# The index add moved to the head of GpSimd's chunk, and the first chunk's field loads split and reordered

## The reference

```python
e = jnp.stack([tbl_0[ids[:, 0]], ..., tbl_38[ids[:, 38]]], axis=1)      # (2048, 39, 16)
x0 = xk = e
for idx, (W, b) in enumerate(params):                                   # three layers, 128 outputs each
    z = jax.nn.relu(jnp.einsum('bhd,bkd,hks->bsd', x0, xk, W) + b[None, :, None])
    if idx != n_layers - 1:
        half = z.shape[1] // 2
        xk = z[:, :half, :]
        direct.append(z[:, half:, :])
    else:
        direct.append(z)
z = jnp.sum(jnp.concatenate(direct, axis=1), axis=-1)
h = jnp.concatenate([z, dense_ctx], axis=1)
h = jnp.maximum(h @ W_top1 + b_top1, 0.0)
h = jnp.maximum(h @ W_top2 + b_top2, 0.0)
y = h @ W_top3
```

## Time and profile before

| | |
|---|---|
| Time, median of 3 runs | 2474.45 us (2474.23 to 2475.2) |
| The profiled execution | 2474.38 us, of it the span 2472.6 us |
| TensorE (PE) busy | 2373.9 us, 96% |
| TensorE weight loads (PEld) | 1539.6 us, 62% |
| VectorE (DVE) busy | 2212.4 us, 89% |
| ScalarE (ACT) busy | 1364.1 us, 55% |
| GpSimd (POOL) busy | 2155.9 us, 87% |
| DMA, mean over the span | 189 GB/s |
| Granted TensorE clock, mean | 0.995 |

### The profile page before, as it was taken

How to read it: one execution, slowest core, us unless ns; L and a number is a source line. 1 busy time by engine, 2 the same in 40 slices (tenths; PEclk the granted TensorE clock), 3 DMA queues, 4 the chain that set the end, 5 groups by cost and what they waited for, 6 DMA issues and landing times. The chain is left out here.

```text
span 2472.6 us, 32417 instructions
## 1 busy us (share of the span) xinstructions
PE 2373.9 (96%) x8192; PEld 1539.6 (62%) x8192; DVE 2212.4 (89%) x2047; ACT 1364.1 (55%) x1532; POOL 2155.9 (87%) x1350
## 2 busy tenths in 40 slices
PE   1799999999999999999999999999999999999999
PEld 1466666666666666666666666666666666666665
DVE  2689999999999999999999999999999999999983
ACT  2355555555555555555555555555555555555552
POOL 4799999999999999999999999999999999999640
PEclk9899999999999999999999999999999999999999
DMA  7888888888878888888888788888888878888710
GB/s 179 187 187 207 196 185 211 212 173 209 207 186 194 210 209 176 204 211 181 203 204 209 177 204 212 181 206 205 201 180 208 214 177 208 208 188 191 199 55 1
DMA packets 398547, 467.04 MB, mean 189 GB/s; under 512 B 170337, under 2 KB 179553, under 8 KB 398257
## 3 DMA queue, kind: packets, MB, share of 16 engines
q1 hardware_dynamic: 299202, 302.30, 54.3%
q10 hardware_dynamic: 78848, 159.39, 24.7%
q0 software_dynamic: 20480, 5.15, 1.8%
HBM read 457.03 MB, written 9.71 MB: 189 GB/s over the span
## 5 line engine op out<-in xcount | busy, mean ns | idle before, releaser
L458 POOL TENSOR_TENSOR low<-prod_pool,high 128x1024 fp32r<-128x1024 f32 (+1 forms) x640 | 1532.5, 2395 | 88.8 <-ACT high L775 73.2
L775 ACT ACTIVATE high<-prod_pool 128x1024 fp32r<-128x1024 f32 (+1 forms) x640 | 677.3, 1058 | 733.5 <-DVE prod_pool L516 695.9
L627 PE MATMUL z<-prod_whole,w_whole 128*128 128x512 f32 (+1 forms) x2176 | 1011.5, 594 | 5.6 <-DVE prod_whole L516 5.6
L627 PE MATMUL z<-high,w_high 128*128 128x512 f32 (+1 forms) x1920 | 939.5, 489 | 55.9 <-ACT high L775 55.9
L627 PE MATMUL z<-high,w_low 128*128 128x512 f32 (+1 forms) x1920 | 758.6, 395 | 0.0
L429 POOL DMA_INDIRECT rows<-table,index x640 | 611.5, 955 | 147.8 <-issue 99.0
L516 DVE TENSOR_TENSOR prod_whole<-xh,x 128x1024 f32<-128x1024 f32 x512 | 620.5, 1212 | 110.1 <-PE z L627 90.8
L627 PE MATMUL z<-low,w_high 128*128 128x512 f32 (+1 forms) x1920 | 614.0, 401 | 33.5 <-POOL low L458 33.3
L627 PEld LDWEIGHTS z<-prod_whole,w_whole 128*128 128x128 f32 (+1 forms) x2176 | 412.7, 190 | 355.7 <-issue 296.8
L516 DVE TENSOR_TENSOR prod_pool<-xh,x 128x1024 f32<-128x1024 f32 x512 | 621.3, 1213 | 10.0 <-POOL low L458 10.0
L627 PEld LDWEIGHTS z<-high,w_high 128*128 128x128 f32 (+1 forms) x1920 | 363.6, 189 | 229.2 <-issue 141.1
(11 more groups left out here) (45 smaller groups left out, 365.5 us busy)
## 6 DMA issues: line engine op xcount, KB each, us to landing
xh<-x_rows SPq DMA_DIRECT2D x64, 2560.0 KB, 16.5
xh<-x_rows ACTq DMA_DIRECT2D x64, 2432.0 KB, 20.6
xb<-x_rows SPq DMA_DIRECT2D x128, 546.0 KB
xb<-x_rows SPq DMA_DIRECT2D x64, 468.0 KB
xa<-x_rows SPq DMA_DIRECT2D x192, 78.0 KB
rows<-table,index POOLq DMA_INDIRECT x640
x_rows<-rows SPq DMA_DIRECT2D x256, 20.0 KB
xh<-staged SPq DMA_DIRECT2D x2, 1280.0 KB, 6.9
```

Source lines behind the costliest of these rows:

```text
L458: pool.tensor_tensor(low[0:g.rows, g.split_slot, 0:n, :], prod_pool[0:g.rows, g.slot, 0:n, :], high[0:g.rows, g.split_slot, 0:n, :].bitcas ...
L627: return pe.matmul(z[stage][:, :], weights[0:g.rows, table[stage, t], :], src[0:g.rows, i, :], start=t == 0 and weights is not w_low and s ...
L775: act.activation(high[0:g.rows, g.split_slot, 0:n, :], src[0:g.rows, 0:n, :], ACT.Copy).then_inc(high_ready, 1)
```

## The change

Two things, both in the order of work and in what is waited for; no computation is added or dropped.

First, `begin_gather` is cut in two. `make_index` holds the waits for the ids and for the stored rows and the add; it runs at the head of GpSimd's chunk, before the first low part. `begin_gather` keeps the wait for the add's semaphore and runs where it ran. Chunk 0 makes two indices; only the first one moves.

Second, in chunk 0 alone: ScalarE copies xa before it asks for the odd fields, no longer after; odd and even fields are each asked for in two parts, tiles 0 to 9 and the rest, with a semaphore of its own for the first parts (`first_fields_loaded`); VectorE starts stage 1 when the first parts are in, and waits for the rest at the group that begins with tile 10.

```diff
+        first_fields_loaded = sem("first_fields_loaded")
...
-        def load_fields(engine, c, p, hh):
+        def load_fields(engine, c, p, hh, loaded, first=0, end=TK):
...
-            n = (F + 1 - hh) // 2
-            spread = bass.AP(tensor=col.tensor, offset=col.offset + hh * step,
-                             ap=[[0, H], [2 * step, n], [1, CN]])
-            engine.dma_start(xh[p][hh * H:(hh + 1) * H, 0:n, :], spread).then_inc(xh_loaded[p], 16)
+            end = min(end, (F + 1 - hh) // 2)
+            spread = bass.AP(tensor=col.tensor, offset=col.offset + (2 * first + hh) * step,
+                             ap=[[0, H], [2 * step, end - first], [1, CN]])
+            engine.dma_start(xh[p][hh * H:(hh + 1) * H, first:end, :], spread).then_inc(loaded, 16)
+
+        def load_first_fields(engine, hh):
+
+            load_fields(engine, 0, 0, hh, first_fields_loaded, end=TK // 2)
+            load_fields(engine, 0, 0, hh, xh_loaded[0], first=TK // 2)
...
-                load_fields(sp, c, p, 0)
+                if known and c == 0:
+                    load_first_fields(sp, 0)
+                else:
+                    load_fields(sp, c, p, 0, xh_loaded[p])
...
-            def begin_gather(c, p):
-
-
+            def make_index(c, p):
                 pool.wait_ge(ids_loaded[p], 8 * (c - p) + 16)
+                if not isinstance(c, int) or c >= 2:
+
+                    pool.wait_ge(stored[p], 8 * STORES * (c - p))
                 pool.tensor_tensor(index[p][:, :], ids_sb[p][:, :], row_base_sb[:, :],
                                    ALU.add).then_inc(index_ready, 1)
-                if not isinstance(c, int) or c >= 2:
-
-                    pool.wait_ge(stored[p], 8 * STORES * (c - p))
+
+            def begin_gather(c):
                 pool.wait_ge(index_ready, c + 1)
...
+                if gathers:
+                    make_index(*gathers[0])
                 for i, (g, at) in enumerate(mine):
                     low_parts(g, at)
                     for _ in range(-(-len(left) // (len(mine) - i))):
                         at, q, j = left.pop(0)
                         if j == 0:
-                            begin_gather(at, q)
+                            if at is not gathers[0][0]:
+                                make_index(at, q)
+                            begin_gather(at)
                         gather(q, j)
...
+                    if second and g.tiles[0] == TK // 2:
+                        second()
...
-                dve.wait_ge(xh_loaded[p], 16 * (c - p) + 32)
+                begun = isinstance(c, int) and c == 0
+                if begun:
+                    dve.wait_ge(first_fields_loaded, 32)
+                else:
+                    dve.wait_ge(xh_loaded[p], 16 * (c - p) + 32)
...
-                products(1, c, xh[p], xk[0], None if begun else lambda: sum_last(c - 1, 1 - p))
+                products(1, c, xh[p], xk[0], None if begun else lambda: sum_last(c - 1, 1 - p),
+                         (lambda: dve.wait_ge(xh_loaded[p], 32)) if begun else None)
...
-            load_odd_fields(0, 0)
             copy_xa(0)
+
+            load_first_fields(act, 1)
             round_stage(0, 0)
```

More of the change, by code:

```diff
@@ L468, in _ @@
             for c in range(2):
-                begin_gather(c, c)
+                make_index(c, c)
+                begin_gather(c)
                 for j in range(GATHERS):
@@ L493, in low_parts, with products @@
                 ).then_inc(low_by_dve, 1)
-            def products(stage, c, spread, shared, after=None):
+            def products(stage, c, spread, shared, after=None, second=None):
                 owed = None
                 for g in groups(stage, c):
+                    if second and g.tiles[0] == TK // 2:
+                        second()
                     if g.kind == WHOLE:
@@ L555, in chunk @@
             def chunk(c, p):
-                dve.wait_ge(xh_loaded[p], 16 * (c - p) + 32)
+                begun = isinstance(c, int) and c == 0
[3 more added lines that the diff above has]
+                    dve.wait_ge(xh_loaded[p], 16 * (c - p) + 32)
                 dve.wait_ge(relu_done[0], 3 * c + 2)
-                begun = isinstance(c, int) and c == 0
-                products(1, c, xh[p], xk[0], None if begun else lambda: sum_last(c - 1, 1 - p))
+                products(1, c, xh[p], xk[0], None if begun else lambda: sum_last(c - 1, 1 - p),
+                         (lambda: dve.wait_ge(xh_loaded[p], 32)) if begun else None)
                 if not (isinstance(c, int) and c == CHUNKS - 1):
@@ L796, in load_odd_fields @@
                     act.wait_ge(pads_cleared, 2)
-                load_fields(act, c, p, 1)
+                load_fields(act, c, p, 1, xh_loaded[p])
             def chunk(c, p):
```

## The result

The changed kernel takes 2451.47 us (median of 4 runs, 2449.94 to 2452.91) against 2474.82 us for the kernel before on the same chip (2474.23 to 2475.57): a ratio of 0.9905, with a 95% interval of 0.9888 to 0.9923. The forecast was 2449.5 us. The profiled execution took 2451.39 us, its span is 2449.6 us, 23.0 less than before, and the granted TensorE clock is 0.994 on average, 0.995 before.

The account below looks back on a forecast made before the run. The bound was taken to be a two-chunk loop through four engines, 36.18 us a chunk. From 2474.4 us, 23.9 for the moved index add and 1.0 for the start gave 2449.5 us, range 2444 to 2457.

Parts of the forecast that it names:

- GpSimd's piece: GpSimd's stretch of the four-engine loop, head's low part to TensorE's low part: 20.94 us, forecast to lose 0.78.
- The pause: Gather behind the chunk's first low part stands still 0.81 us instead of 0.16; taken as waiting for the add's result.
- The rival in which the pause stays: The 0.81 us before the first gather remains, saving only 5 us: 2469.5 us, chance 0.10.
- The pair: First low part to first gather on GpSimd: 3.34 us, forecast to fall by 0.78 to 2.56.
- the chain: Two-chunk loop of five legs through TensorE, ScalarE, VectorE and GpSimd: 72.37 us, forecast 71.59, or 35.80 a chunk.
- The moved add: Index add at the head of GpSimd's chunk, forecast hidden under the wait for the rounding; without that cover, 0.21 us.
- GpSimd's own loop: GpSimd's work per chunk without its wait at the head: 36.10 us, forecast to fall by 0.78 to 35.32.
- the room: Time GpSimd reaches the head before the rounding is done, forecast at 0.48 us with the moved add counted.
- The start: First chunk's reordering: chunk 1 between 2 us sooner and 5 us later, taken as 1 us of gain.
- The rival in which it reaches the end: Chunk 1's rows stored 11 us sooner, the start's gain adding to the forecast: 2439 us, chance 0.07.
- The slower rival: Head waits for stored rows, blocking low parts, if they land over 15.7 us later: 2511 us, chance 0.07.
- TensorE's pace: Rival: every chunk falls to TensorE's own 35.51 us, saving 40 us: 2434.5 us, chance 0.06.

Follow-up runs that it names:

- e6: Kernel before with only the index add moved to the head, plus the gather behind the fifth low part moved behind the sixth: 2445.68 us, ratio 0.9885.
- e2: Kernel before with only the first chunk's reordering, the index add left behind the first low part: 2476.66 us, ratio 1.0008.
- e5: Kernel before with only the index add moved to the head, plus six spare integer adds there that nothing reads: 2487.65 us, ratio 1.0052.
- e7: Changed kernel with chunk 1's rows stored between the two parts of chunk 0's even fields, not behind both: 2449.76 us, ratio 0.9902.
- e4: Kernel before with only the index add moved to the head, plus the gather behind the fifth low part moved behind the tenth: 2462.71 us, ratio 0.9949.
- e11: Kernel before with only the index add moved to the head, plus the gather behind the third low part moved behind the tenth: 2449.81 us, ratio 0.9902.
- e3: Kernel before with only the index add moved to the head, plus two spare integer adds there that nothing reads: 2449.91 us.
- e10: Kernel before with only the index add moved to the head, first chunk as before, run beside the changed kernel: 2450.31 us, ratio 0.9899.
- e9: The changed kernel run once more without any edit, beside the index add alone: 2450.42 us, ratio 0.9902.

## Why the prediction was right

**The bound.** Right: 36.19 to 35.77 us a chunk was seen, 35.80 was forecast; what was taken out of GpSimd's piece came off the pace at half its size, four of the five legs did not move, and e6, which took a gather out of the piece, went faster still. The ground that the forecast gave was weaker than it thought: "the loop's sum fits the pace to 0.01 us" holds for any path of two chunks. The waits at the hand-overs, which it also read, are what carries it.

**The pause.** Right: the first gather now starts 0.15 us after the low part, so the 0.81 us was waiting for the add's result. The Trainium skill (GPSIMD Engine Reference, 2.1 Instruction dispatch) has completion gate only what waits on the semaphore. With that the trace agrees: 2.51 us from the low part to the gather with the index long made, 3.34 without, and e2 has the 0.81 back, while a low part, which does not wait for the add, starts 0.17 us after the add's start (121.88, 122.05). The rival in which the pause stays fell, and with it 2469.5 us.

**The size.** From chunk 1 to chunk 60 the forecast counted 23.9 us, 23.4 for the steady chunks and 0.5 for chunk 1; there they are 24.2. The pair fell by 0.83 rather than 0.78 and the chain by 0.81, of which 30 turns are 24.3. That 2449.5 came within 2 us of 2451.47 is in part luck: in the profiled execution the start was 2.8 us later, where 1 us of gain was counted, and the end 1.6 us sooner, where nothing was.

**The moved add.** The sum was right, its reason mis-sized. "GpSimd's own loop falls to 36.10 - 0.78 = 35.32, which counts the moved add already" was the step that failed. The 0.78 was the difference of two pairs, and the add's own time was in it; at the head that time comes back, 0.17 us. With the measured pair, 36.10 - 0.83 + 0.17 = 35.44, and e5 gave 35.48. So the room is 0.30 and not 0.48, and the wait at the head 0.13 and not 0.5. The add still cost nothing, since 0.17 is under 0.30; a step of 0.4 us, which the forecast would have called hidden, would have cost 0.1 us a chunk, as an estimate from the room of e5.

**The start.** The forecast took 1 us of gain, between 2 us sooner and 5 us later. Measured beside its partner the reordering is worth nothing (2450.42 against 2450.31). Two steps were off. The copy of xa was put near 34, 11 us after its request, from a steady chunk in which xa and xb are alone; here the even fields stand right behind them in the same queue, and it came after 15.9; that they are the cause is likely, but no run takes them away. And SyncE's even fields did not end sooner: chunk 1's xa was asked for 38.6 us after chunk 0's (62.77 - 24.13), 37.5 before. What was right is that the first layer's head start would be lost; that it is lost because the same bytes have to pass fits e7, but is not shown apart from that. The rival in which it reaches the end (2439) fell; its mark was chunk 1's xa copied before 76. The copy came at 86.06, where the forecast had it near 82. A rule of the Trainium skill spoke against this part (DMA: Bandwidth & Descriptors, Rules for kernel authors: issue early, wait late). The late request does show as 10.5 us of waiting on VectorE at 56.47; no run here shows that it costs time in the end.

**The slower rival.** In the steady chunks no idle time of GpSimd at the head ends with a transfer; the stored rows were there.

**TensorE's pace.** It was not reached. Other loops stand close behind the one that the change shortened (71.56 us for two chunks), as the runs with moved gathers show: one of 35.72 us for one chunk in e6, one of 72.05 and 71.60 for two in e4 and e11; and GpSimd's own is at 35.48. The forecast knew only of the one that it shortened, GpSimd's own and TensorE's. Nor is TensorE's 35.51 the same everywhere: the stretch behind the last gather, without a wait too, took 35.25 us in e5 (2359.61 to 2394.86) and 35.24 in e3, against 35.49 to 35.52 in the other kernels; no run shows why.

## What to carry to other kernels

Where no engine is full, look for a loop through several engines: start at the small wait that comes once per round, follow it to where the same wait returns, and check at each hand-over that the engine which takes over had been waiting. A sum that fits the pace is no proof, since every such path has it. What is taken from any leg is worth that much per turn, until the next-longest loop takes over. A step whose result the next one waits for costs its own time and the time to hand the result over (0.2 and 0.8 us here); moved ahead of unrelated work, only its own time is left, and that has to be added again where it now stands. Before moving work out of one loop, list the loops that pass through the place where it goes, with the wait that each has to spare.

## What the runs showed of the hardware that I had not expected

An index add of 128 by 10 integers took 0.22 us on GpSimd, and another behind it only 0.16 to 0.17 more (six in 0.98). What made it dear was the hand-over to the gather, 0.81 us, on the same engine; a gather behind unrelated work starts after 0.16, and one right behind another gather after 0.30 (1031.57 and 1032.83 in e6).

Transfers on one queue slow those that are asked for on another at the same time: from request to copy, xa and xb took 22.7 us in the kernel before, with the odd fields asked for on ScalarE's queue beside them, and 22.7 in e10; with those asked for only after the copy they took 15.9 in the changed kernel and 14.9 in e9. The even fields followed on their own queue in all four.
